# A fused attention and expert layer on one core: score products taken alternately from both halves of the heads, and all orders laid out anew

## What is computed

```python
h = take(table, x, axis=0)                        # (8, 1024, 256) float32
n = layernorm(h)
qkv = n @ qkv_proj.T + qkv_bias                   # q, k, v: 16 heads of 16
attn = softmax(0.25 * q @ k.T)                    # 8 x 8 scores for each column and head
h = h + (attn @ v) @ out_proj.T + out_bias
n = layernorm(h)
scores = sigmoid(n @ Wg.T)                        # 16 experts, 4 groups: best 2 groups, best 4 experts
cw = 2.5 * normalised weights of the chosen 4
hid_e = relu(n @ W1_e.T) ** 2                     # 16 experts and a shared pair, 128 wide each
out = h + sum_e cw_e * (hid_e @ W2_e.T) + shared
```

## Time and profile before

| | us |
|---|---|
| runs: median (lowest to highest) | 1297.54 (1296.45 to 1298.26) |
| the profiled execution | 1296.51 |
| its span, first to last instruction | 1294.7 |
| mean granted TensorE clock | 0.995 of full |

### The profile page before, as it was taken

The page is one execution under the profiler, slowest core; times in us unless marked ns, Lnnn a source line. Parts: engine busy times, 40 slices in busy tenths (PEclk is TensorE's granted clock), DMA queues, the critical chain, the costliest instruction groups (busy, mean ns, idle before and its releaser), DMA issues.

```text
span 1294.7 us, 19965 instructions
## 1 busy us (share of the span) xinstructions
PE 1259.3 (97%) x7556; PEld 1037.6 (80%) x7556; DVE 1022.7 (79%) x1732; ACT 591.2 (46%) x1040; POOL 500.2 (39%) x717
## 2 busy tenths in 40 slices
PE   4798999999999999999999999999999999999998
PEld 3467889797888979788797888979788797888987
DVE  4989787887878789787878878788787878978754
ACT  5234445444554544454353544544355354444443
POOL 6437254161623507253260724416262360705100
PEclk9899999999999999999999999999999999999999
DMA  6002222121321212122121322212122120212131
GB/s 217 1 17 83 66 83 82 35 82 49 99 66 55 94 33 97 52 83 82 34 86 45 100 66 82 71 46 82 50 89 76 51 92 29 94 49 83 66 107 57
DMA packets 34128, 91.66 MB, mean 71 GB/s; under 512 B 4720, under 2 KB 13296, under 8 KB 34032
## 3 DMA queue, kind: packets, MB, share of 16 engines
q1 hardware_dynamic: 30960, 81.99, 19.0%
q0 software_dynamic: 3072, 8.39, 2.5%
HBM read 81.46 MB, written 8.91 MB: 70 GB/s over the span
## 4 chain that ended last, share of the span: by engine, by line
PE 94%; DVE 3%; issue 1%; ACT 1%; POOL 1%; DMA 0%; DVEq 0%; POOLq 0%; SPq 0%
PE psY L1157 32%; PE psH L1142 30%; PE psB L1188 10%; PE psB L1203 9%; PE psA L1233 4%; PE psB L1221 2%; PE psA L1221 2%; PE psA L1245 2%; PE psB L1174 1%; PE psA L1174 1%; DVE ring L771 1%; PE psA L1254 1%; PE psY L1261 0%; DVE stats L754 0%; POOL xin L399 0%
## 5 line engine op out<-in xcount | busy, mean ns | idle before, releaser
L1157 PE MATMUL psY<-w_hi,hid_hi 128*128 128x256 f32 x1152 | 328.5, 285 | 0.0
L1157 PE MATMUL psY<-w_hi,hid_lo 128*128 128x256 f32 x1152 | 324.5, 282 | 0.0
L1157 PE MATMUL psY<-w_lo,hid_hi 128*128 128x256 f32 x1152 | 323.6, 281 | 0.0
L733 DVE SCALAR_TENSOR_TENSOR r_sb<-psH,cwB 128x512 f32<-128x512 f32 x256 | 174.8, 683 | 113.7 <-PE psH L1142 102.9
L533 ACT ACTIVATE hid_hi<-r_sb 128x512 fp32r<-128x512 f32 x288 | 179.8, 624 | 181.4 <-PE psY L1157 181.4
L1157 PEld LDWEIGHTS psY<-w_hi,hid_hi 128*128 128x128 f32 x1152 | 217.3, 189 | 31.4 <-issue 23.5
L1142 PE MATMUL psH<-xT_hi,w_hi 128*128 128x512 f32 x576 | 229.2, 398 | 1.4 <-DVE r_sb L733 1.4
L1142 PE MATMUL psH<-xT_hi,w_lo 128*128 128x512 f32 x576 | 227.4, 395 | 0.0
L1142 PE MATMUL psH<-xT_lo,w_hi 128*128 128x512 f32 x576 | 227.3, 395 | 0.0
L531 ACT ACTIVATE p_sb<-r_sb 128x512 f32<-128x512 f32 x288 | 180.2, 626 | 101.8 <-DVE r_sb L733 94.6
L1157 PEld LDWEIGHTS psY<-w_lo,hid_hi 128*128 128x128 f32 x1152 | 216.9, 188 | 8.1
(11 more groups left out here) (136 smaller groups left out, 1980.6 us busy)
## 6 DMA issues: line engine op xcount, KB each, us to landing
cwB<-cw_dram SPq DMA_DIRECT2D x128, 512.0 KB, 3.9
out<-h SPq DMA_DIRECT2D x32, 256.0 KB, 3.2
xin<-table,idx POOLq DMA_INDIRECT x64
ring<-w_t SPq DMA_DIRECT2D x4, 256.0 KB, 5.3
h<-w_t SPq DMA_DIRECT2D x2, 512.0 KB, 8.5
ring<-w_t SPq DMA_DIRECT2D x1, 512.0 KB, 5.9
p_sb<-w_t SPq DMA_DIRECT2D x2, 256.0 KB
cwB<-w_t SPq DMA_DIRECT2D x1, 512.0 KB
```

The costliest lines, as they stand in the source:

```text
L733: nc.vector.scalar_tensor_tensor(r_sb[:, n % 2, :], psH[:, n % 2, :], 0.0, cwB[:, (r // QN) % 2, r % QN, :], ALU.max, ALU.mult).then_inc(w ...
L1157: last = nc.tensor.matmul(psY[:, j // 2, (j % 2) * D:(j % 2 + 1) * D], hid[a][:, e % R, j * P:(j + 1) * P], W2[b][:, e, :], start=(e == 0 ...
```

## The change

- `product_on` numbers the products the other way: t = 2*lp + ih, so that they alternate between the halves.
- `score(blk, lp)` is now one call for two positions and both halves: it waits for a product of each half and issues four strips. There are 4 calls for 8.
- The order of calls is laid out anew in all engines' lists, in the period and in the prologue. No work is added or left out; of the 17 calls `warm(4)` in the prologue seven now stand ahead of the first transpose (before: one).

The core of the diff:

```diff
@@ product_on
-            lp, ih = t % LP, t // LP
+            lp, ih = t // KH, t % KH
@@ POOL, period
                     rstd_of(1, b + 1)
+                    root_of_sum(b + 1)
                 if b + 3 < B:
                     gather(b + 3)
-                if b + 1 < B:
-                    root_of_sum(b + 1)
                 if b + 2 < B:
                     sum_of(b + 2, 0)
+                    bias_in(b + 2)
                     sum_of(b + 2, 1)
-                    bias_in(b + 2)
@@ PE, score
-            def score(blk, t):
-                lp, ih = t % LP, t // LP
-                pe.wait_ge(prod_ready[ih], nth(blk, LP, lp + 1))
-                if t == 0:
+            def score(blk, lp):
+                for ih in range(KH):
+                    pe.wait_ge(prod_ready[ih], nth(blk, LP, lp + 1))
+                if lp == 0:
                     if blk == 0:
                         pe.wait_ge(const_step, CONST_SMALL)
                     pe.wait_ge(qkv_ready, nth(blk, 6, 5))
-                for li in range(2):
-                    row = 64 * ih + 32 * li
-                    last = nc.tensor.matmul(psB[row:row + 32, 0, :], head_sum[:, lp, :], ring[:, t % 4, li, :],
-                                            start=(lp == 0), stop=(lp == LP - 1))
-                last.then_inc(score_mm, 1)
+                for ih in range(KH):
+                    for li in range(2):
+                        row = 64 * ih + 32 * li
+                        last = nc.tensor.matmul(psB[row:row + 32, 0, :], head_sum[:, lp, :],
+                                                ring[:, (KH * lp + ih) % 4, li, :],
+                                                start=(lp == 0), stop=(lp == LP - 1))
+                    last.then_inc(score_mm, 1)
```

More of the change, by code:

```diff
@@ L504, in _ @@
             rstd_of(1, 0)
+            root_of_sum(0)
             gather(2)
-            root_of_sum(0)
+            bias_in(1)
             sum_of(1, 0)
             sum_of(1, 1)
-            bias_in(1)
             for b in range(B + 1):
@@ L907, in period @@
                     norm_stats(0, b + 2)
+                if b > 0:
+                    add_experts(b - 1)
+                if b + 1 < B:
+                    weighted_values(b + 1, 2)
                 if b < B:
@@ L972, in period @@
                 if b < B:
-                    hidden_lo(b, 11)
-                    hidden_lo(b, 12)
+                    hidden_lo(b, 10)
+                if b + 2 < B:
+                    product(b + 2, 2)
                 if b + 1 < B:
                     route(b + 1, 0)
+                if b < B:
+                    weigh(b, 13)
+                if b + 1 < B:
                     route(b + 1, 1)
@@ L1061, in _ @@
             product(0, 7)
+            norm_stats(0, 1)
+            scores_max(0)
+            scores_sum(0)
+            probs_low(0)
             weight_lo(9)
-            scores_max(0)
-            weight_lo(10)
-            scores_sum(0)
-            weight_lo(11)
-            probs_low(0)
-            norm_stats(0, 1)
             weighted_values(0, 0)
@@ L1082, in _ @@
             attention_lo(0, 0)
+            attention_lo(0, 1)
+            transposed_lo(0, 1)
+            weight_lo(10)
+            weight_lo(11)
+            residual(0)
+            weight_lo(12)
             product(1, 0)
-            attention_lo(0, 1)
             product(1, 1)
@@ L1114, in _ @@
             route(0, 17)
+            scores_max(1)
             route(0, 18)
             route(0, 19)
+            hidden_lo(0, 0)
             route(0, 20)
             route(0, 21)
+            scores_sum(1)
+            weight_lo(13)
             probs_low(1)
-            hidden_lo(0, 0)
             weighted_values(1, 0)
-            weight_lo(13)
             weighted_values(1, 1)
@@ L1308, in period @@
                 if b < B:
+                    down(b, 8)
                     up(b, 11)
-                    down(b, 9)
+                if b + 2 < B:
+                    qkv(b + 2, 2)
+                if b < B:
                     up(b, 12)
@@ L1313, in period @@
                     transpose_rows(1, b + 1)
-                if b + 2 < B:
-                    qkv(b + 2, 2)
                 if b < B:
                     up(b, 13)
-                    up(b, 14)
+                if b + 2 < B:
+                    qkv(b + 2, 3)
+                if b < B:
+                    down(b, 9)
                 if b + 1 < B:
@@ L1330, in period @@
                     score(b + 2, 1)
+                if b < B:
+                    up(b, 15)
+                    down(b, 11)
+                    down(b, 12)
+                    up(b, 16)
+                if b + 2 < B:
                     score(b + 2, 2)
@@ L1374, in _ @@
             qkv(0, 4)
+            qkv(0, 5)
             score(0, 0)
@@ L1406, in _ @@
             qkv(1, 2)
-            out_projection(0)
             qkv(1, 3)
@@ L1410, in _ @@
             score(1, 0)
+            transpose_rows(1, 0)
             score(1, 1)
+            qkv(1, 5)
+            logits(0)
             score(1, 2)
-            score(1, 3)
-            score(1, 4)
-            score(1, 5)
-            transpose_rows(1, 0)
-            score(1, 6)
-            score(1, 7)
-            logits(0)
             warm(4)
             up(0, 0)
-            qkv(1, 5)
-            warm(4)
+            score(1, 3)
             up(0, 1)
             up(0, 2)
+            weights_transpose(0)
             warm(4)
-            weights_transpose(0)
+            warm(4)
             spread_probs(1, 0)
```

246 lines of the change are left out of this document (110 added, 136 removed).

## The result

The change makes the kernel slower: 1317.4 us median (1311.6 to 1318.6) against 1297.9 us for the kernel before on the same chip, a ratio of 1.0146 with a 95% interval of 1.0117 to 1.0174. The forecast was 1252. The profiled execution took 1311.6 us with a span of 1309.6, against 1294.7 before. It is the fastest of the four; the other three took 1316.6 to 1318.6, and what these lost besides is in no trace.

What follows compares the result with a forecast made beforehand. PE was taken to bound the periods, busy in all 77.07 us; DVE, ACT and POOL latencies decide the first 104 us. Span 1294.7 - 41.6 (periods) - 4 (prologue) = 1249.1, plus 1.8 and 1.0: 1252 us; range 1241 to 1275.

Steps and rivals of the forecast that it cites:

- Part 1: PE's score products in the periods: four-strip calls at 0.86 us each save 3.43 us a period, 48 us in 14 periods.
- Part 2: DVE in the periods: keeps up; 17.2 us of work before scores_max, probabilities ready 0.2 us before PE's spread 0.
- Rival B: DVE becomes the bound in the periods: 1.5 us more in each, 75.6 with the gather's wait, 1273 us; chance 0.19.
- Part 3: POOL in the periods: root_of_sum ahead of gather(b + 3) causes 0.45 us of new waits a period, between 0 and 1.5.
- S: Start of DVE's scores_max in a period, forecast 18.15 us after the end of qkv(b2, 3) on PE.
- a margin of 0.4: At down(b1, 0) in a period: inputs ready at K + 34.6 us, PE there at K + 35.0, K being qkv(b2, 3)'s end.
- Rival D: Slower: the gather behind the root lands late, sharing DMA engines with loads; decides from 6.5 us landing; 1321 us, chance 0.05.
- POOL's second wait: out_projection in a period waits for POOL's late sums; forecast ready at K + 56.0 us (K: qkv(b2, 3)'s end), as PE arrives.
- Part 4: The prologue: reordered calls make it 4 us shorter, between 0 and 7, with out_projection(0) some 6 us earlier.
- The end: What follows the scores' last period: no change, 0 us within 1.
- The stated signs: Changed profile: 16-instruction score groups of about 1.85 us, periods 73.6 to 74.5; particular waits would point to particular causes.

## Why the prediction was wrong

- **Part 1 held.** Price of a period's score calls, from start to next call: 7.12 us before and 3.71 after, 3.41 saved where 3.43 was forecast. The rest of a period grew by 0.4, so that it lasts 74.07 without waits instead of 73.63. The run with a call between the halves shows that the mechanism is the overlap. The Trainium skill (TensorE: Matmul & The Clock Gate, "Measured speedup vs the span model") has three strips lose a fifth of the ideal against one, from which the prediction made an estimate of 1.08 a call; here eight old calls took 7.12 and four new ones 3.71, 0.89 and 0.93 each, so the measurement decides against that estimate (no run here has a single strip, so the page's own figure is not tested).
- **Part 2 held.** From `product(b + 2, 1)` to `scores_max` DVE took 17.13 us (forecast 17.2); `spread_probs(b + 2, 0)` waits nowhere in the periods. Rival B is out.
- **Part 3 is the step that failed**, in its size. The mechanism was named, with the two loads in the same microseconds; its price was not believed. The landing was taken from a prologue row at 2.70; beside the loads it was 4.5 to 6.4, mostly above 5. The prediction's own allowance, that the gather lands like the loads, was 1.2 more; it was 1.8 to 3.7 more. The root took 1.50 instead of 1.08 and the issues 5.18 instead of 4.85, so the last issue came 0.7 late as well. By the prediction's own sum with these terms: ready at S + 11.8 + 5.7 + 2.7 = S + 20.2, PE there at S + 17.4 in the trace (S + 16.9 in the forecast), a wait of 2.8 where the trace has 2.87. I took 0.45 for it, and the cost as one that only bites beyond a margin of 0.4. The kernel before had the gather landing in 2.9 to 4.9 in its periods, with 35 us to spare; that was in the trace and not read.
- **What was not priced at all is the second-order cost**: at the end of nine of PE's 11 waits the clock falls, which costs 1.6 us. The prediction spoke of the clock only for the prologue. Waits of 28.6 and falls of about 16 (8 x 1.6 and a double one of 3.0) together make up 44 of the 47 us by which the periods miss the forecast (1085.5 against 1079.8 - 41.6). The whole span misses it by 60.5 (1309.6 against 1249.1): the prologue has 10.6 of this and the end 2.4. Rival D had the right place, but its point of decision (a landing of 6.5) left out the clock and a longer prologue; with them 5.7 was enough.
- **POOL's second wait** came as forecast: `out_projection` waited 0.65 to 0.68 in two periods, those that start without a wait for the gather.
- **Part 4 had the wrong sign**, a second step that failed: 4 us less were forecast and it became 6.6 more. It priced DVE's and PE's moves as if POOL's instructions kept their length (`rstd_of(1, 0)`, 3.2 before, took 7.0). Its largest term, `out_projection(0)` some 6 earlier because the qkv calls no longer stand before it, came out at 1.9 (68.5 for 70.4): the call was waiting for the attention of block 0, and now the qkv calls wait behind it. It had the clock fall only between the spreads, where the clock cost nothing that can be told, and not ahead of `down(0, 0)`. How the loss divides among these stays open.
- **The end** was taken as 0, within 1; it grew by 2.4, of which 1.1 is the new wait for `o_sb`.
- **The stated signs held**: groups of 1.92, a wait of `down` for `add_experts` with the statistics waiting for `xin`. They named the cause in the first reading of the trace. The prediction also said that it is wrong if the statistics wait over 4 us: in the periods with the wait they did, 4.2 to 6.1.

## What to carry to other kernels

Moving a transfer from a place with 35 us of slack to one with none changes its price: read its landing beside the transfers that will be in flight there, not where it once ran alone. When PE is made to wait on the chain, add what the clock takes after the wait. Tiny instructions on POOL that head a chain are stretched by DVE's large two-input instructions beside them; here keeping DVE idle undid the stretch, but the transposes behind it came only 0.4 us earlier. And a call moved ahead of others on an in-order list is only earlier if its inputs are: otherwise the others wait with it.

## What the hardware showed that was not expected

- Matmuls of free column strips start ahead of earlier ones whose strip is busy: half 1's first one started third, with eight issued ahead of it, and the group took 1.94 us instead of 1.92.
- A gather of four indirect transfers lands 2.7 us after its last issue alone, 4.5 to 6.4 with two 512 KB loads issued 0.1 to 0.7 us behind it, mostly 3.5 to 3.9 (at most 5.4) with a load issued 0.9 ahead of it (the run with the gather first).
- A POOL instruction of 128x4 takes 0.20 us alone and 1.0 to 1.2 beside DVE's products; in the other direction, a DVE split of 1.22 us took 2.5 beside POOL's `bias_in`.
- The granted clock fell at the end of waits of PE in the middle of a run, nine times out of 11 (these nine lasted 2.2 to 3.5 us, the two others 1.65 and 2.61), though PE had been busy for some 75 us on either side, and ten times out of 11 in the run with the prologue of before; the waits of 0.65 and 0.68 for `out_projection`, and those of 1.18 in the old order with four strips, were followed by none.
